# Tridiagonalization of a 256 x 256 matrix: from a row form with a full update at every step to a column form with panels of 16

## What is computed

```python
def _L1_gnn_ref(features, A, W1, b1, W2, b2):
    deg = jnp.sum(A, axis=0) + jnp.sum(A, axis=1) - jnp.diagonal(A)
    d_inv_sqrt = jnp.where(deg > 0, jax.lax.rsqrt(deg), 0.0)
    L = jnp.diag(deg) - A
    L_norm = d_inv_sqrt[:, None] * L * d_inv_sqrt[None, :]
    _, U = jnp.linalg.eigh(L_norm)
    agg = jnp.einsum('mn,bnd->bmd', U.T, features)
    h = jax.nn.relu(agg @ W1 + b1)
    out = h @ W2 + b2
    return jnp.einsum('nm,bmd->bnd', U, out)
```

## Time and profile before

| | |
|---|---|
| time, median of 2 | 3251.84 us |
| profiled execution: span | 3248.8 us |
| busy in the span | PE 53%, PE weight load 44%, VectorE 78%, ScalarE 29%, GpSimd 8% |
| reduction, 22.8 to 1469.3 us | 1446.5 us, 45% of the span |
| of it two tiles, to 850.8 | 828.0 us, VectorE busy 784.3 |
| one tile, to 1467.0 | 616.2 us, VectorE busy 535.7 |
| all behind it | 1779.5 us |

### The profile page before, as it was taken

The page is one execution under the profiler, slowest core; times in us unless marked ns, Lnnn a source line. Parts: engine busy times, 40 slices in busy tenths (PEclk is TensorE's granted clock), DMA queues, the critical chain, the costliest instruction groups (busy, mean ns, idle before and its releaser), DMA issues. The chain is left out here.

```text
span 3248.8 us, 43582 instructions
## 1 busy us (share of the span) xinstructions
PE 1708.6 (53%) x7118; PEld 1442.9 (44%) x7118; DVE 2519.9 (78%) x15298; ACT 947.0 (29%) x3429; POOL 255.4 (8%) x367
## 2 busy tenths in 40 slices
PE   5555555555544444441000004057697788788777
PEld 4445554554433344441000003046476676677666
DVE  7999999999988888889999999967544544554553
ACT  2222222222232222222000001035244344344334
POOL 0000000000000000003222223001100000000000
PEclk9999999999999999997555556578798898888888
DMA  0000000000000000001000000001000000000000
GB/s 24 0 0 0 0 0 0 0 0 0 0 0 0 0 0 0 0 0 43 0 1 0 1 1 1 1 20 64 26 9 5 13 13 0 13 13 0 13 6 6
DMA packets 22932, 22.29 MB, mean 7 GB/s; under 512 B 1584, under 2 KB 19664, under 8 KB 22736
## 3 DMA queue, kind: packets, MB, share of 16 engines
q1 hardware_dynamic: 20304, 13.28, 1.4%
q0 software_dynamic: 2560, 8.39, 0.7%
HBM read 13.28 MB, written 8.39 MB: 7 GB/s over the span
## 5 line engine op out<-in xcount | busy, mean ns | idle before, releaser
L267 PE MATMUL bank<-const,row 1*128 1x1 f32 x766 | 202.9, 354 | 408.2 <-DVE row L410 407.3
L267 PEld LDWEIGHTS bank<-const,row 1*128 1x128 f32 x766 | 181.2, 314 | 430.5 <-DVE row L410 429.0
L280 PE MATMUL bank<-A,onehot 128*128 x508 | 223.7, 542 | 264.1 <-DVE A L437 261.1
L287 PE MATMUL bank<-A,ucol 128*128 x762 | 285.6, 512 | 0.0
L677 DVE SCALAR_TENSOR_TENSOR q<-rec,nb,q 128x14 f32<-128x14 f32 (+1 forms) x1270 | 277.3, 257 | 0.0
L1409 ACT ACTIVATE gate<-bank,gbias 128x128 f32<-128x128 f32 (+3 forms) x576 | 209.0, 432 | 177.8 <-PE bank L1364 137.2
L673 DVE RECIPROCAL rec<-q 128x14 f32<-128x14 f32 (+1 forms) x1270 | 247.6, 236 | 11.8 <-DVE q L677 1.4
L280 PEld LDWEIGHTS bank<-A,onehot 128*128 128x128 f32 x508 | 127.1, 311 | 284.4 <-issue 284.4
L320 ACT ACTIVATE nrm<-n,tiny 128x1 f32<-128x1 f32 x254 | 74.8, 294 | 545.1 <-DVE n L426 545.1
L287 PEld LDWEIGHTS bank<-A,ucol 128*128 128x128 f32 x762 | 223.5, 325 | 16.4 <-DVE ucol L455 0.2
L784 PE MATMUL bank<-tq,const 128*128 128x1 f32 x2 | 0.6, 363 | 367.2 <-DVEq L864 367.2
(11 more groups left out here) (375 smaller groups left out, 4893.4 us busy)
## 6 DMA issues: line engine op xcount, KB each, us to landing
xnext<-in_x SPq DMA_DIRECT2D x16, 256.0 KB, 3.6
x_scratch<-x1out POOLq DMA_DIRECT2D x16, 256.0 KB, 3.8
xin<-x_scratch SPq DMA_DIRECT2D x16, 256.0 KB, 2.8
out<-yout POOLq DMA_DIRECT2D x16, 256.0 KB, 2.6
const<-in_consts SPq DMA_DIRECT2D x1, 1619.5 KB, 6.6
adjN<-in_adj SPq DMA_DIRECT2D x1, 256.0 KB, 7.1
wqkv<-in_L_gnn_Wqkv SPq DMA_DIRECT2D x1, 192.0 KB, 7.3
W<-in_L_gnn_W SPq DMA_DIRECT2D x2, 64.0 KB, 3.2
```

Source lines behind the costliest of these rows:

```text
L267: last = mm(pCol[:, 0, t:t + 1], row[0:1, t * P:(t + 1) * P], ones[0:1, 0:1], start=True, stop=True)
L280: mm(pNext[:, 0, 0:width_], onehot[:, :].broadcast_to([P, P]), A[:, (k0 + 1) // P, window], start=True, stop=True).then_inc(h_next, 1)
L287: last = mm(pAu[:, 0, 0:width_], ucol[:, t:t + 1].broadcast_to([P, P]), A[:, t, window], start=(t == tiles[0]), stop=(t == tiles[-1]))
```

## The change

The reduction is written anew; what stands ahead of it and behind it only follows in names and in the constants' layout (two more columns in `ident` and `below`, the table `pick` gone).

- Columns take the place of rows. The current column `x` and a unit vector `e` stand in `R[:, :, 0:2]`, one or two elements per partition.
- `A` stays as it is for `PANEL = 16` steps. Each step leaves a pair of vectors (u, p) in `R` and a pair in `Pe`; the products with `A` that a step needs are corrected by dot products with the pairs so far (`Ec`, `Cc`, L380 and L387). After 16 steps TensorE turns both panels (four transposes for two tiles), VectorE and ScalarE copy them out, TensorE multiplies them, and VectorE takes the product from `A` in one subtraction (L445).
- Every product with `A` is now the matrix tile as stationary operand against two moving columns, `[x e]` (L297): four matmuls for two tiles, one for one tile.
- The norm of `x`: TensorE turns the column to a row on every partition (L286, 128 moving columns per tile), ScalarE copies it out of PSUM (L331), VectorE squares and sums it (L384), ScalarE takes the root and a half of it (L333, L334).
- The steps are 256, in two phases of 128 (two tiles, then one), each a loop of 8 turns over a body of 16 steps on every engine. A second small block behind finds which steps had a nonzero rest and sets the signs of `e`.

```diff
-STEP = 32
-UNROLL = 4
+PANEL = 16
+        PHASES = ((0, (0, 1)), (P, (1,)))
+        BLOCKS = P // PANEL
 # TensorE
-                for k0, k1, width_, tiles in SEGMENTS:
-                    with nc.tensor.Fori(k0, k1) as k:
...
+                for first, tiles in PHASES:
+                    with nc.tensor.Fori(0, BLOCKS) as blk:
+                        for j in range(PANEL):
+                            k = blk * PANEL + (first + j)
+                            w = 2 * j
+                            if j:
+                                pe.wait_ge(h_e, k + 1)
+                                pe.wait_ge(h_p, k)
+                                heads = tiles if j == PANEL - 1 else tiles[0:1]
+                                for t in heads:
+                                    mm(dots[:, 1, XE:XE + w], R[:, t, 1:2].broadcast_to([P, P]), R[:, t, XE:XE + w],
+                                       start=(t == heads[0]), stop=(t == heads[-1]))
+                            pe.wait_ge(h_e, k + 1)
+                            pe.wait_ge(h_x, k + 1)
+                            for t in tiles:
+                                last = mm(pRow[:, t * P:(t + 1) * P], R[:, t, 0:1].broadcast_to([P, P]), ident1, start=True, stop=True)
+                            last.then_inc(h_row, 1)
+                            for t in tiles:
+                                last = mm(dots[:, 0, 0:XE + w], R[:, t, 0:1].broadcast_to([P, P]), R[:, t, 0:XE + w],
+                                          start=(t == tiles[0]), stop=(t == tiles[-1]))
+                            last.then_inc(h_D, 1)
+                            if j == 0:
+                                pe.wait_ge(h_A, blk + (first // PANEL + 1))
+                            for u in tiles:
+                                for t in tiles:
+                                    last = mm(pZ[:, u, :], A[:, t, u * P:(u + 1) * P], R[:, t, 0:XE],
+                                              start=(t == tiles[0]), stop=(t == tiles[-1]))
+                            last.then_inc(h_z, 1)
+                            pe.wait_ge(h_q, k + 1)
+                            for t in tiles:
+                                last = mm(pG[:, :], ones, Qp[:, t, :, :].rearrange("p a b -> p (a b)"), ...)
+                            last.then_inc(h_g, 1)
+                        ...
+                        for t in tiles:
+                            nc.tensor.transpose(pPd[0:2 * PANEL, 0, t * P:(t + 1) * P], R[:, t, XE:XE + 2 * PANEL], ident1)
+                        for t in tiles:
+                            last = nc.tensor.transpose(pPe[0:2 * PANEL, 0, t * P:(t + 1) * P], Pe[:, t, :], ident1)
+                        last.then_inc(h_T, 1)
+                        pe.wait_ge(h_Tc, blk * 2 + (2 * first // PANEL + 2))
+                        for t in tiles:
+                            last = mm(pDelta[:, t, c0:N], PeT[:, t * P:(t + 1) * P], PdT[:, c0:N], start=True, stop=True)
+                        last.then_inc(h_dl, 1)
 # ScalarE, each step
+                            act.wait_ge(h_row, k + 1)
+                            A_(xrow[:, here0:N], pRow[:, here0:N], ACT.Copy).then_inc(h_rowc, 1)
+                            act.wait_ge(h_n2, k + 1)
+                            A_(nrm[:, :], n2[:, :], ACT.Sqrt, bias=tiny[:, :]).then_inc(h_nrm, 1)
+                            A_(half_n2[:, :], n2[:, :], ACT.Copy, scale=0.5).then_inc(h_nrm, 1)
...
 # VectorE, each step
-                            v.scalar_tensor_tensor(A[:, t0, window], pAu[:, 0, 0:width_], acol[:, t0:t0 + 1], A[:, t0, window], ...)
...
+                            i_xm = ch.mark(v.tensor_tensor(xm[:, here], x, below_h, ALU.mult))
+                            dve.wait_ge(h_D, k + 1)
+                            i_sgn = ch.mark(v.tensor_scalar(sgn[:, :], x0, 0.0, 0.5, ALU.is_lt, ALU.subtract))
+                            i_E = ch.mark(v.tensor_tensor(Ec[:, here, :, 0:w], ...))
+                            dve.wait_ge(h_rowc, k + 1)
+                            v.tensor_tensor_reduce(row2[:, c0:N], xrow[:, c0:N], xrow[:, c0:N], 1.0, 0.0, ALU.mult, ALU.add, n2[:, :]).then_inc(h_n2, 1)
+                            i_C = ch.mark(v.tensor_reduce(Cc[:, here, :], Ec[:, here, :, 0:w], AX.X, ALU.add))
+                            dve.wait_ge(h_nrm, k * 2 + 2)
+                            i_n2s = ch.mark(v.tensor_tensor(n2s[:, :], n2[:, :], sgn[:, :], ALU.mult))
+                            i_inv = ch.mark(v.reciprocal(inv[:, :], nrm[:, :]))
+                            i_nrms = ch.mark(v.tensor_tensor(nrms[:, :], nrm[:, :], sgn[:, :], ALU.mult))
+                            dve.wait_ge(h_z, k + 1)
+                            i_zr = ch.mark(v.tensor_tensor(zr[:, here, :], pZ[:, here, :], Cc[:, here, :], ALU.subtract))
+                            ...
+                            scaled(x, xmA[:, here], xAu[:, :], zzm[:, here]).then_inc(h_x, 1)
+                            ...
+                            scaled(Pe[:, here, w + 1], u, k2[:, :], p).then_inc(h_w, 1)
+                        dve.wait_ge(h_T, blk + (first // PANEL + 1))
+                        v.tensor_copy(PeT[:, c0:N], pPe[0:2 * PANEL, 0, c0:N]).then_inc(h_Tc, 1)
+                        dve.wait_ge(h_dl, blk + (first // PANEL + 1))
+                        v.tensor_tensor(A[:, here, c0:N], A[:, here, c0:N], pDelta[:, here, c0:N], ALU.subtract).then_inc(h_A, 1)
```

More of the change, by code:

```diff
@@ L13 @@
 T2 = N // P
-STEP = 32
-AW = N + STEP
-UNROLL = 4
-SEGMENTS = []
-for k_first, k_end, tiles in ((0, P - 1, (0, 1)), (P - 1, N - 2, (1,))):
-    for k0 in range(k_first, k_end, STEP):
-        k1 = min(k0 + STEP, k_end)
-        whole = k1 - (k1 - k0) % UNROLL
-        SEGMENTS += [(a, b, N - 1 - a, tiles) for a, b in ((k0, whole), (whole, k1)) if b > a]
+PANEL = 16
+PAD = 2
 NODES, CH, BATCH = 256, 128, 32
@@ L41, in constants @@
     x = r ^ j
+    wide_j = np.arange(N + PAD)[None, None, :]
     parts = {
-        "ident": r == j, "below": r > j, "above": r < j, "pick": np.tile(np.eye(P), (1, T2)),
+        "ident": r == wide_j, "below": r > wide_j, "above": r < j,
         "level": np.where(x > 0, np.floor(np.log2(np.maximum(x, 1))), -1),
@@ L253, in build @@
[L253 to L258 removed]
+        XE = 2
@@ new lines, in build @@
+        R = sb("R", [P, T2, XE + 2 * PANEL])
+        Pe = sb("Pe", [P, T2, 2 * PANEL])
+        PeT = sb("PeT", [2 * PANEL, N])
+        PdT = sb("PdT", [2 * PANEL, N])
+        xm = sb("xm", [P, T2])
+        xmA = sb("xmA", [P, T2])
+        Ec = sb("Ec", [P, T2, 2, 2 * PANEL])
+        Cc = sb("Cc", [P, T2, 2])
+        zr = sb("zr", [P, T2, 2])
+        Qp = sb("Qp", [P, T2, 2, 2])
+        Au = sb("Au", [P, T2])
+        rc = sb("rc", [P, T2])
+        zz = sb("zz", [P, T2])
+        zzm = sb("zzm", [P, T2])
@@ new lines, in build @@
+        tiny = sb("tiny", [P, 1])
+        stat = sb("stat", [P, 2])
+        sigma, beta = stat[:, 0:1], stat[:, 1:2]
+        xrow = sb("xrow", [P, N])
+        row2 = sb("row2", [P, N])
+        kept = sb("kept", [P, N, 2])
+        square = sb("square", [P, N])
+        flip = sb("flip", [P, N])
+        n2, half_n2, nrm, sgn, n2s, nrms, inv, hh1, hh, rsig, crd, xAu, v1, uAu, k2, nbeta = (sb(n, [P, 1]) for n in
+            ("n2", "half_n2", "nrm", "sgn", "n2s", "nrms", "inv", "hh1", "hh", "rsig", "crd", "xAu", "v1", "uAu", "k2", "nbeta"))
@@ L324, in _ @@
                 v = nc.vector
-                def cut(first, end, n):
-                    size = -(-(end - first) // n)
-                    return [(i, min(i + size, end)) for i in range(first, end, size)]
-                v.memset(tiny[:, :], 1e-35)
-                v.memset(u_rel[:, :], 0.0)
-                v.memset(ucol[:, :], 0.0)
-                v.memset(kept[:, :, :], 0.0)
-                v.memset(row[:, :], 0.0).then_inc(h_end, 1)
-                dve.wait_ge(h_end, 1)
-                dve.wait_ge(h_first, 1)
@@ L378, in _ @@
+                dve.sem_inc(h_A, 1)
+                for first, tiles in PHASES:
                     here = slice(tiles[0], T2)
-                    t0, t1, nt = tiles[0], tiles[-1], len(tiles)
-                    pieces = cut(0, width_, 2 * len(tiles))
-                    steps = min(UNROLL, k1 - k0)
-                    with v.Fori(0, (k1 - k0) // steps) as turn_:
+                    nt = len(tiles)
+                    with v.Fori(0, BLOCKS) as blk:
                         dve.sem_clear(h_step)
@@ new lines, in _ @@
+                v.memset(eRow[:, :], 0.0)
+                v.memset(Hrow[:, N - 1:N], 0.0)
+                v.memset(flip[:, 0:1], 1.0)
+                v.tensor_tensor(scratch[:, :, 0:N - 1], V[:, :, 0:N - 1], later[:, :, 1:N], ALU.mult).then_inc(h_end, 1)
+                dve.wait_ge(h_end, 2)
+                v.tensor_tensor(scratch[:, :, 0:N - 1], scratch[:, :, 0:N - 1], scratch[:, :, 0:N - 1], ALU.mult).then_inc(h_end, 1)
+                dve.wait_ge(h_end, 3)
+        with nc.Block() as block:
```

(20 more changed lines are left out.)

306 lines of the change are left out of this document (104 added, 202 removed).

## The result

The changed kernel takes 3284.49 us (median; 3284.08 to 3284.9) against 3251.84: ratio 1.0101, 95% interval 1.0085 to 1.0118. It is 32.6 us slower, where +69 was forecast. The profiled execution has a span of 3283.2 us.

The account below looks back on a forecast made before the run. VectorE bounds the old reduction; the change leaves a ring through three engines. Steps 1429.8 us, panel ends 82, front 0.3, behind 7: reduction 1519 against 1446.5, +73, taken as +69; with 3.0 for the median, 3321 us, range 3265 to 3355.

Parts of the forecast that it names:

- The two-tile step: First phase: 3.89 us from x to zr, then 2.39 us of VectorE's work to the next x, 6.28 in all.
- the price of a row matmul: TensorE, front of a step: the first matmul with 128 moving columns takes 0.79 us, and 0.14 stays in front of a queue.
- The one-tile step: Second phase: the norm is last, nrms awaited and sigma follow, then the chain from Qp on takes 2.18: 4.89 us.
- Which wait comes last: Two tiles: products with A come last, by half a microsecond; one tile: the norm, at 2.24 us against 1.75.
- The panel's end: After 16 steps: two-tile subtraction starts at 4.77 us, one-tile at 2.9; long VectorE branch, 5.6 and 5.1 us per turn.
- rival 1: VectorE's turn between panels is cheap or hidden: 26 us less, 3295 us; chance 0.13.
- Rival 2: VectorE's small operations are cheaper than read, two scalars at 0.13 us: 3277 us; chance 0.12.
- Rival 3: TensorE pays one record for a two-column product: 63 and 55 us less, 3203 us; chance 0.05.
- Rival 4: Unseen waits in the ring, 0.1 to 0.2 us a step: 3345 to 3370 us; chance 0.17.
- Rivals 5 and 6: 5: TensorE falls to 1.2 GHz, 3465 us, chance 0.03. 6: ring is VectorE's work alone, 2750 us, chance 0.05.
- my own case: Whole kernel: every term of the sum lies within its reading, 3300 to 3345 us; chance 0.45.
- The end: Behind the reduction's steps: memsets, two passes over V, block changes, matmuls and four awaited operations, 7 us.

Follow-up runs that it names:

- the kernel with the rows kept: Changed kernel with the squared norm taken from the dots' first column; TensorE still does the 128-column row matmuls, whose result nobody reads: 3242.4 us.

## Why the forecast was too high, step by step

- **The two-tile step, 6.28 against 6.10.** The failed step is the price of a row matmul: "0.79, 0.21 more, of which about 0.07 is its drain and 0.14 stays in front of a queue". The earlier trace rows shows a lone 128-column matmul, with nothing queued behind it; it can't show what a queue pays, and I set that at its upper end without a bound of its own. Measured: nothing. From the end of x (64.99) to zr (68.72) it is 3.73 instead of 3.89. The tail from zr to the next x's end is 2.37, forecast 2.39. That width is what costs nothing, and not the row matmul itself, is shown by the kernels with 4 and with 128 columns: 3244.0 and 3242.4 us, steps 6.10 in both.
- **The one-tile step, 4.89 against 4.77.** The same term: the sign starts 1.18 behind the end of x (1110.10 to 1111.28), not 1.31; n2s 2.10 behind it, not 2.24.
- **The sum of it:** 0.14 x 256 = 36 us, nearly the forecast's whole distance of 36.5 us. That it fits so closely is luck, for the smaller errors cancel: 0.04 more in the two-tile steps (-5), 0.02 less in the one-tile steps (+3), one-tile turns 0.5 cheaper (-3), the last step of each one-tile panel 0.4 longer (+3), the 4 us that I had taken off for rounding (+4), and a median that stands 1.3 us above the profiled span and not 3.0 (-2).
- **Which wait comes last** was right in both parts: zr waits for L297 with two tiles, n2s for ScalarE with one, and the kernel with the rows kept moved one part only.
- **The panel's end:** subtraction at 4.58 behind the end of x, forecast 4.77 (the same 0.14 isn't in it; its parts are each a little cheaper); xm 3.33 behind the subtraction's start, forecast 3.5; extras 5.6 and 4.6, forecast 5.6 and 5.1. VectorE idles 2.5 to 2.8 us at a two-tile turn and 3.0 to 3.2 at a one-tile turn, where the forecast wanted over 3 at all 14. The short turn that rival 1 needed would have given 4.4 and 2.5 (forecast 4.2 and 2.8), 7 x 1.2 + 7 x 2.1 = 23 us less (forecast 26), but no turn of the changed kernel was short. The row that I read as a turn of the short loop, 0.70 us idle at 462.86, is the step from one segment's loop into the next; its turns idle 0.8 to 0.9. No term of the sum hung on it.
- **Rival 2** (two scalars cheap) falls: xAu starts 0.20 ahead of v and each takes 0.27 to 0.28. **Rival 3** falls: L297 has two records for each matmul. **Rival 4** (unseen waits) had it the wrong way round. **Rivals 5 and 6** had no part (the 2750 of rival 6 was also too low for its own 3.6 us a step, which with the forecast's panel ends gives some 2815). The result, 3284, lies in the range of 3265 to 3355 but 16 us below my own case's 3300 to 3345, which took the 0.14 for certain.
- **The end:** 6.9 us against 7.

The change itself lost for the reason given: it takes 241 us of VectorE's work away with two tiles and 30 with one, and puts a ring through three engines in its place that is, panel ends included, 3 us shorter with two tiles and 32 us longer with one. The panel ends cost 78 us in all, and the row matmuls another 0.85 a two-tile step for a norm that the dots already held.
